# Low parts of eleven weight chunks by a negated high part and an adding DMA

## The reference

```python
x = x + attn(layernorm(x), wq, wk, wv, wo)      # 16 query heads, 4 key/value heads of 128, rotary positions
x = x + ffn(layernorm(x), W1, W2, W3)           # W2 @ hadamard(silu(W1 x) * (W3 x)), 1024 hidden

scores = einsum('bhid,bhjd->bhij', qi, ki) * diag[None]      # decay mask, no softmax
kv = blk * kv + einsum('bhjd,bhje->bhde', ki * k_dec, vi)    # state over chunks of 64
```

## Time and profile before

| | |
|---|---|
| median of 3 runs | 270.7 us (270.65 to 270.79) |
| span of the profiled execution | 269.5 us |
| PE busy | 261.0 us (97%) |
| PE weight loads | 227.4 us (84%) |
| DVE busy | 204.9 us (76%) |
| ACT busy | 167.7 us (62%) |
| POOL busy | 143.9 us (53%) |
| DMA | 13.23 MB moved, most of it in the first 40 us |

### The profile page before, as it was taken

How to read it: one execution, slowest core, us unless ns; L and a number is a source line. 1 busy time by engine, 2 the same in 40 slices (tenths; PEclk the granted TensorE clock), 3 DMA queues, 4 the chain that set the end, 5 groups by cost and what they waited for, 6 DMA issues and landing times.

```text
span 269.5 us, 4222 instructions
## 1 busy us (share of the span) xinstructions
PE 261.0 (97%) x1506; PEld 227.4 (84%) x1506; DVE 204.9 (76%) x336; ACT 167.7 (62%) x283; POOL 143.9 (53%) x105
## 2 busy tenths in 40 slices
PE   7898799999999999999999999999999999999995
PEld 5786488979889888888889889898888879988895
DVE  4799899899979897869899799795575984143333
ACT  3879896875898767556867768984353542043230
POOL 2302989888889467532795897899519200000000
DMA  6594620211220000000020001200000000100002
GB/s 205 189 346 169 243 80 2 78 31 47 80 78 4 0 1 0 4 0 0 2 61 17 2 11 67 80 2 2 0 0 2 0 0 21 59 0 2 0 0 78
DMA packets 5635, 13.23 MB, mean 49 GB/s; under 512 B 624, under 2 KB 2544, under 8 KB 5616
## 3 DMA queue, kind: packets, MB, share of 16 engines
q1 hardware_dynamic: 5040, 12.39, 13.4%
q10 hardware_dynamic: 576, 0.59, 0.6%
HBM read 11.93 MB, written 1.05 MB: 48 GB/s over the span
## 4 chain that ended last, share of the span: by engine, by line
PE 72%; DVE 15%; ACT 5%; issue 4%; DMA 2%; POOL 1%; SPq 0%; DVEq 0%; ACTq 0%
PE bank L317 24%; PE bank L318 24%; PE bank L319 23%; DVE rope_b L1014 2%; DVE rope_a L1013 2%; DMA w_raw<-in_wq 2%; DVE bank L1041 2%; DVE v_hid L1000 1%; PE bank L333 1%; ACT rope_b L661 1%; ACT rope_b L660 1%; DVE qk L1021 1%; DVE rope_b L1065 1%; DVE o_lo L1051 1%; DVE p_lo L1046 1%
## 5 line engine op out<-in xcount | busy, mean ns | idle before, releaser
L843 POOL TENSOR_TENSOR qk<-rope_a,rope_b 128x512 f32<-128x512 f32 x36 | 49.7, 1383 | 25.6 <-DVE rope_b L1014 25.1
L317 PE MATMUL bank<-xt_hi,w_hi 128*128 128x512 f32 x140 | 55.0, 393 | 0.5 <-issue 0.4
L318 PE MATMUL bank<-xt_lo,w_hi 128*128 128x512 f32 x140 | 54.7, 391 | 0.0
L319 PE MATMUL bank<-xt_hi,w_lo 128*128 128x512 f32 x140 | 54.5, 389 | 0.0
L850 POOL TENSOR_TENSOR q_hid<-qk,q_hid 128x512 fp32r<-128x512 f32 x29 | 39.8, 1379 | 10.4 <-ACT q_hid L666 10.4
L673 ACT ACTIVATE p_hi<-bank 128x512 fp32r<-128x512 f32 x48 | 28.6, 596 | 15.7 <-DVE bank L1041 15.2
L1014 DVE TENSOR_TENSOR rope_b<-rope_b,sin_sb 128x512 f32<-128x512 f32 x40 | 37.7, 942 | 0.0
L318 PE MATMUL bank<-w_lo,o_hi 128*128 128x256 f32 x128 | 36.2, 283 | 0.0
L319 PE MATMUL bank<-w_hi,o_lo 128*128 128x256 f32 x128 | 36.2, 283 | 0.0
L317 PE MATMUL bank<-w_hi,o_hi 128*128 128x256 f32 x128 | 36.1, 282 | 0.0
L1013 DVE TENSOR_TENSOR rope_a<-bank,cos_sb 128x512 f32<-128x512 f32 x40 | 27.5, 687 | 10.6 <-ACT rope_b L661 10.1
(11 more groups left out here) (90 smaller groups left out, 614.8 us busy)
## 6 DMA issues: line engine op xcount, KB each, us to landing
w_raw<-in_w SPq DMA_DIRECT2D x6, 512.0 KB, 3.2
decay_sb<-in_decay SPq DMA_DIRECT2D x4, 512.0 KB, 5.3
w_raw<-in_wo SPq DMA_DIRECT2D x4, 512.0 KB, 4.7
w_raw<-in_wq SPq DMA_DIRECT2D x3, 512.0 KB, 3.3
x_sb<-in_x SPq DMA_DIRECT2D x3, 256.0 KB, 7.1
out<-x_sb SPq DMA_DIRECT2D x6, 128.0 KB, 1.8
w_raw<-in_wv SPq DMA_DIRECT2D x1, 512.0 KB, 6.1
w_raw<-in_wk SPq DMA_DIRECT2D x1, 384.0 KB, 6.4
```

The source lines that it names most:

```text
L317: pe.matmul(o, a_hi, b_hi, start=first, stop=False, skip_group_check=shared)
L318: pe.matmul(o, a_hi, b_lo, start=False, stop=False, skip_group_check=shared)
L319: return pe.matmul(o, a_lo, b_hi, start=False, stop=last, skip_group_check=shared)
L843: pool.tensor_tensor(qk[:, r % 2, :], rope_a[:, r % 2, :], rope_b[:, r % 2, :], ALU.add).then_inc(rope_sum_pool, 1)
```

## The change

For chunks 3 to 13 (`ADDED`) the low part is no longer a subtraction on DVE or POOL. ACT, right behind the high part, copies it once more with a factor of -1 into `w_lo` (`minus_high`). POOL then issues a DMA that reads the chunk from DRAM a second time and adds it onto `w_lo` (`add_weights`). PE waits for that DMA's semaphore at the first use, and the slot of `w_raw` is free for its next load when the high part has been written.

```diff
-LOW_ON_DVE = (0, 3, 5, 7)
+LOW_ON_DVE = (0,)
+ADDED = range(3, 14)
@@ wait_low_weights(engine, n)
-            if n in LOW_ON_DVE:
+            if n in ADDED:
+                engine.wait_ge(w_added[n], 16)
+            elif n in LOW_ON_DVE:
@@ sync: load_chunk(n)
-                if n >= SLOTS:
+                if n - SLOTS in ADDED:
+                    sp.wait_ge(w_hi_done, n - SLOTS + 1)
+                elif n >= SLOTS:
@@ scalar
+            def minus_high(n):
+                _, _, at = CHUNKS[n]
+                act.wait_ge(w_hi_done, n + 1)
+                act.activation(w_lo[:, at:at + CH], w_hi[:, at:at + CH].bitcast(F32), ACT.Copy,
+                               scale=-1.0).then_inc(w_minus, 1)
...
             high_weights(3)
+            minus_high(3)
             high_weights(4)
+            minus_high(4)
...
             high_weights(5)
+            minus_high(5)
             high_weights(6)
+            minus_high(6)
...
             high_weights(7)
+            minus_high(7)
             high_rope(("K", 0, 1))
...
             high_weights(8)
+            minus_high(8)
...
                     high_weights(unit_chunk(u))
+                    minus_high(unit_chunk(u))
@@ gpsimd
+            def add_weights(n):
+                w, j, at = CHUNKS[n]
+                pool.wait_ge(w_minus, n - ADDED.start + 1)
+                pool.dma_start(w_lo[:, at:at + CH], dram[w][j], accum_op=ALU.add).then_inc(w_added[n], 16)
...
             low_weights(1)
             low_weights(2)
+            add_weights(3)
+            add_weights(4)
             rope_add(("Q", 0, 3))
-            low_weights(4)
             low_rope(("Q", 0, 3))
+            add_weights(5)
...
             rope_add(("Q", 0, 6))
-            low_weights(6)
+            add_weights(6)
...
             rope_add(("Q", 0, 8))
+            add_weights(7)
...
-            low_weights(8)
+            add_weights(8)
...
-                if unit_chunk(u) is not None and unit_chunk(u) not in LOW_ON_DVE:
-                    low_weights(unit_chunk(u))
+                if unit_chunk(u - 1) is not None and u > FIRST_UNIT:
+                    add_weights(unit_chunk(u - 1))
@@ vector
             rotate(("Q", 0, 2))
-            low_weights(3)
             rope_add(("Q", 0, 2))
...
             rotate(("Q", 0, 5))
-            low_weights(5)
...
             rotate(("K", 0, 2))
-            low_weights(7)
...
-                if unit_chunk(u) in LOW_ON_DVE:
-                    low_weights(unit_chunk(u))
```

More of the change, by code:

```diff
@@ L195, in build @@
         w_hi_done, had_done = sem("w_hi_done"), sem("had_done")
+        w_minus = sem("w_minus")
+        w_added = {n: sem(f"w_added{n}") for n in ADDED}
         w_lo_dve, w_lo_pool = sem("w_lo_dve"), sem("w_lo_pool")
```

## The result

The changed kernel takes 287.75 us (median of 4 runs, 286.24 to 288.02) against 270.67 us before: a ratio of 1.0614, 95% interval 1.0597 to 1.0631. It is 17.1 us slower, where 6.5 us had been forecast with a range up to 282.5. The span of the profiled execution is 286.2 us, 269.5 before.

What follows compares the result with a forecast made beforehand. PE bounds from 57 us on; before that DVE and ACT are full. Late landing +3.8, three ACT passes +3.15, slack 0.06, given back 0.4: +6.5 us on 270.7, so 277.2 us, range 273.0 to 282.5.

Steps and rivals of the forecast that it cites:

- ACT's lateness: Added passes on ACT: +2.1 us at `attend(0, 0)` from chunks 3 and 4, 3.15 us to the key tile from chunks 5 to 7.
- the low end of its own range: Forecast's own range, low end: 275.3 us if the add of chunk 3 lands within 4.8 us, sum given as +4.6.
- the crowded row: Add of chunk 3: 6.5 us to landing, from a plain load issued behind three others; landing at 30.9, `attend(0, 0)` +4.0 us.
- the 9 us that had been named as a sign against the prediction: First use of chunk 3: prediction wrong if PE waits there less than 4 us or over 9; about 6 expected.
- The prediction's sentence on the Trainium skill's rule: Adding transfers move at about half rate: landing of chunk 3 up to 3.2 us later, end at up to 280.4 us.
- the bound of 10 us: Add of chunk 3: upper bound on issue to landing if other transfers queue ahead, landing at 34.4.
- slow adds: Rival at chunk 3's first use: adds take 10 us or more, or issuing holds POOL over 2.3 us; 280.7 us, chance 0.17.
- the 0.4 that was not given back: PE's 0.7 us wait at 55 us: shorter DVE operations give back between 0 and 0.7 us, taken as 0.4.
- no busier: POOL: each DMA issue, between 0.33 and 2.3 us, replaces a 2.3 us subtraction, so POOL gets no busier.
- For chunks 8 to 13 the price was 0: ACT passes of late chunks: hidden, tightest slack 1.3 us against 1.05 at the low scores; uncovered, up to 6.3 us.
- New PE waits in units 12 to 14: Late units: new PE waits there would show the prediction wrong; it expected no PE waits after 60 us.
- The 1.8 us wait for the low scores: PE's longest early wait; rival "Faster" had idle time shrink by up to 2.4 us through less DVE work, 268.3 us, chance 0.05.

Runs made afterwards that it cites:

- e2: Kernel before plus the eleven negated copies on ACT, written to a tile nobody reads, low parts as before, no adding DMA: 279.52 us, ratio 1.0329.
- e6: Changed kernel with the same eleven POOL DMAs as plain copies without the add (low parts wrong): 284.63 us, ratio 1.0514.
- e5: Changed kernel, but SP issues the load of chunk 5 and everything behind it only after the add of chunk 3 has landed: 282.96 us, ratio 1.0440.
- e3: Changed kernel with 40 dummy matmuls on PE ahead of the first use of chunk 3: 284.15 us, ratio 1.0491.
- e10: e1 with the negated copies of chunks 6 and 7 moved into ACT's idle time in unit 1: 276.63 us, ratio 1.0217.
- e4: Kernel before with only chunks 8 to 13 made by negated copy and adding DMA: 273.25 us, ratio 1.0090.
- e7: e4 with the negated copies of chunks 9 to 13 moved to the end of the next unit's list on ACT: 271.75 us, ratio 1.0044.
- e1: Changed kernel with chunk 3 back on a DVE subtraction, no minus pass or add for it: 279.16 us, ratio 1.0309.
- e11: e8 with chunk 6 made by negated copy and adding DMA: 271.88 us, ratio 1.0040.
- e8: Kernel before with only chunk 5 moved, its high part into ACT's idle time and its low part into DVE's: 273.23 us, ratio 1.0091.

## Why the prediction was wrong

**What held.** PE bound from 57 us on and nothing to gain there; ACT as the engine that decides from 20 to 44 us; DVE's removed pass worth nothing. ACT's lateness was sized right where it was counted: 2.1 us at `attend(0, 0)` and 3.15 us to the key tile, measured 2.1 and 3.2 in e2, alone, where DVE's passes were still in place. Two figures of the prediction are slightly off without moving anything: the low end of its own range adds up to +4.8 and not +4.6, and the product of 1.76 us is 2.6 times the common 0.68, not twice.

**The term that was mis-sized.** "Being alike, the crowded row is the nearer one: I take 6.5 us" was 10.3. The start of the attention was put 4.0 us late and came 10.2 late; the wait of 10.4 us is beyond the 9 us that had been named as a sign against the prediction. The row was of a plain load; two things separate it from the add, and I had priced neither in the sum: the add holds the DMA engines 1.86 times as long (e6, 8.0 us without it), and it shares them with what SP sends, more of it than before (e5, 5.5 us without SP's loads). The prediction's sentence on the Trainium skill's rule had the first, and gave an end at up to 280.4; the bound of 10 us was right for the landing.

**The terms that were missing.** No step counted the granted clock. The rival "slow adds", with its landing at 34.4 (34.5 measured), is the case that came, and its price of 280.7 is 7 us short. 2.2 us of that are the two projections at half clock behind the wait, 1.5 us a second stretch at half clock near 57 us that comes in most runs. e3 shows the first by taking it away; it also lost the second, but as e5's runs show that this one comes and goes, its cause stays open: all I can say is that much the same three waits of PE (0.8, 1.3 and 1.0 us, from 48 to 56 us in the changed kernel) stood ahead of it where it came, and where it did not. Of the rest of the 7 us most are the transposes (2.1) and the 0.4 that was not given back.

Nor did any step count POOL's wait in its own order. The prediction compared how long POOL is held by an issue with the subtraction that goes, and found POOL "no busier". It asked whether the issues of chunks 3 and 4 hold up the sum behind them, but not the one of chunk 5: that one makes POOL wait 3.24 us for ACT, the sum of query tile 4 comes late, and ACT waits 0.50 us for it (1.60 in e10).

**Hidden work that was not hidden.** For chunks 8 to 13 the price was 0, on the low part of the scores with 1.3 us of slack. That slack was there. The late consumer was another: the PSUM bank that the key tile's rotate frees for the norm's transposes. e4 measures 2.4 us for these chunks (273.25 - 270.82; 2.2 on PE), and e7 returns 1.4 to 1.5 by their order on ACT. The page's wait list could not show it, since before PE does not wait there; I should have followed each product of ACT's full stretch, not only the scores. "New PE waits in units 12 to 14" had been named as a sign against the prediction; they stand in units 5 and 13.

**Given back.** 0.4 us had been expected from the wait at 55 us. It is 0.7 us in the changed kernel as before: nothing. The 1.8 us wait for the low scores did vanish under the longer one.

By parts, from the table: 10.0 us the wait for chunk 3, 2.2 us its half clock, 1.9 less for the old wait that it swallowed, 0.5 less up to `project(Q, 0, 6)`, 3.8 us from there to the key tile (three passes of ACT, and its 0.5 us wait for POOL), 1.5 us the second half clock, 2.1 us the transposes: 17.2 us. The parts are not independent: the passes alone cost 8.9 us, with 1.4 us of them a collision that the change removes, and the 2.1 us that they cost at the start lie under the DMA's wait.

## What to carry to other kernels

Price a transfer that gates a matmul by its kind and by what will share the DMA engines at that moment, not by a plain load's row, and give it its time before the first use: here 5.5 us without the crowd and 10.3 in it. A long wait of PE can cost more than its length: here the matmuls behind it ran at half clock, for 2.2 us more. An issue that waits for another engine holds up everything behind it in its own engine's order, however short it is itself. And a pass added to an engine that has no idle time is late for everything that the engine makes afterwards: look for the consumer with the least slack among all of them, PSUM banks to be freed included.

## What the runs showed of the hardware

- A DMA of 512 KB from DRAM that adds onto SBUF landed 5.2 to 5.7 us after its issue with nothing beside it (changed kernel, e4, e5), a copy from the same queue 3.5 to 3.8 (e6), a load from SP's queue 3.3 (median of six); POOL was held 0.86 to 1.06 us by issuing an add and 0.54 to 0.73 us by a copy.
- Adds alone kept the 16 DMA engines busy at 201 GB/s (e5); plain transfers in a crowd moved 414 GB/s (e6).
- The granted clock went from 1.00 to 0.50 near 29 us, after PE had been idle since 24.2 us, and was back at 1.00 before 40 us; with PE busy on dummy matmuls in that time it did not fall (e3). It also fell after waits of at most 1.9 us: in the traces of e1, e2, e7 and e11 between 30 and 36 us, where those of the kernel before and of e10 stay at 1.00. Of 17 runs of the kernel before, three have a mean clock of 0.993 or 0.994 and take 271.2 to 271.4 us, the other fourteen 270.5 to 270.9. In the changed kernel a second stretch at half clock costs 1.5 us in its trace.
- A DVE operation with two SBUF inputs of 0.68 us took 2.45 and 2.87 us when it started 0.5 and 0.1 us after a POOL subtraction of 2.4 us (e2, e8), and ended 0.54 and 0.55 us after it; with that subtraction gone it took 0.68 us (e11).
